# A straight first block with two low parts of weights in it, and a new share-out of the down projection's first low part

## The chip, the cores and the metric

The kernel runs on one core of one Trainium2 chip. The metric is device time in microseconds (us) of one execution; shown is the median of three. Engines: PE is TensorE, DVE is VectorE, ACT is ScalarE, POOL is GpSimd, SP is SyncE, which here only issues DMAs.

## The reference

One transformer block on x of shape (8, 1024, 512), with shared layernorm:

```python
    x = L0_attn_x
    xn = _layernorm(x, axis=-1)
    x = x + _L0_attn_ref(xn, L0_attn_Wq, L0_attn_Wk, L0_attn_Wv, L0_attn_Wog, L0_attn_Wig, L0_attn_big, L0_attn_Wfg, L0_attn_bfg, L0_attn_gamma, L0_attn_Wout) + _L0_ffn_ref(xn, L0_ffn_w_gate, L0_ffn_w_up, L0_ffn_w_down)
```

`_L0_attn_ref` is an mLSTM with 8 heads: q, k, v, an input and a forget gate from xn; a scan over the tokens of each sequence that updates a state C (32 x 64 a head) and a normalizer n with exponential gates under a running maximum; each head's output is normalized, multiplied by sigmoid(xn Wog) and gamma, and projected by Wout. `_L0_ffn_ref` is silu(xn w_gate) * (xn w_up), projected by w_down, with a hidden size of 2048. All in fp32.

## The kernel before

**Precision.** TensorE multiplies in fp16. Each fp32 operand is held as a sum of two fp16 numbers, a high part and a low part, and each product is three matrix products (high x high, high x low, low x high: L1127 to L1129 in `three`). So all weights have to be split once, in a prologue, before the loop over blocks can use them.

**The prologue.** The weights come in 17 pieces, in the order of `GROUPS`: gates, qk, v; g0 to g3 (gate projection); u0 to u3 (up); o; d0 to d3 (down); out. Each piece but gates has 128 x 2048 numbers. SyncE issues the loads. For each group VectorE takes the largest magnitude of each piece (`maximum`), the engines reduce it over the partitions, and `scales` makes a power of two from it. Then for each piece:

- ScalarE makes the high part, `high_part`: the weight times its scale, rounded to fp16 (L610; for `out` four pieces with their own factors, L607). It counts up `w_hi`.
- The low part, scaled weight minus high part, is made in one of three ways. On VectorE by one `scalar_tensor_tensor` that scales and subtracts (`low_part`, L811, L806 for `out`). On GpSimd for the pieces in `POOL_LOW` (`pool_low`, L508): GpSimd only subtracts, so for these ScalarE first scales the fp32 weight in place (L601) and then copies it to fp16 (L603). On TensorE for the pieces in `PE_LOW`: two products put scaled weight minus high part into four PSUM banks (`low_by_pe`, L1164, L1165), and ScalarE copies them out (`low_from_pe`, L616).

The order on each engine is the order of the code; engines meet by semaphores only. The fp32 weights are staged in memory that is free at the time: g in the slots of u, u in the slots of d, o in the slot of out, and d, qk, v and out in the arena, which holds the working tensors of the loop. This is why a piece of d may not be made before the piece of u that is staged in its slot is done (`wait_split` in `high_part`), and why before the loop VectorE, ScalarE and GpSimd wait for the last low part, that of `out`.

**The loop.** 32 blocks of 256 tokens, four to a sequence. Each engine has a loop of its own over the blocks (`Fori`), with its instructions in a fixed order. In a block TensorE computes gates, q, k, v, then 16 hidden pieces `ffn0` to `ffn15`, each with its gate and up product and, two pieces later, its down product (`down`). The table `AFTER` says which steps of the mLSTM come behind which piece: `es` the scores, `pv` their product with v and the state update, `center`, `scale` and `heads` the normalization of the output, `o` the output gate, `hoT` the turned output, `att` the projection by `out`. Three PSUM banks go round (`USES`, `BANK`): a product may begin when the use of its bank before has been drained. The first uses are gates, q, k; the next, v0, needs the bank of gates, which ScalarE (L656) and VectorE (L942) drain together. A hidden piece goes TensorE, ScalarE (tanh, L690), VectorE (L985, L988), ScalarE (high part, L694), GpSimd (low part, L560), TensorE (`down`).

Of the kernel before, what the change touches and what calls it, by code (L numbers as in the profile page):

```python
# [25 lines left out]
P = 128  # L26
# [98 lines left out]
POOL_LOW = [("qk", 0), ("v", 0), ("g", 0), ("g", 2), ("u", 0)]  # L125
PE_LOW = [("g", 1), ("g", 3), ("u", 1), ("u", 3)]
# [11 lines left out]
def low_done(piece):  # L138

    before = ORDER[:ORDER.index(piece) + 1]  # L140
    for own in (POOL_LOW, PE_LOW):
        if piece in own:
            return len([p_ for p_ in before if p_ in own])
    return len([p_ for p_ in before if p_ not in POOL_LOW and p_ not in PE_LOW])

# [24 lines left out]
def mlstm_mlp_kernel(nc, x, w_dram, gate_bias, gamma, out):  # L170
    ctx = ExitStack()
    with ctx:
# [92 lines left out]
        stage["out", 0] = in_arena(1)  # L265
# [36 lines left out]
        small = sb("small", [P, 112], F32)[:, :]  # L302
# [4 lines left out]
        m_carry = small[0:NH, 96:97]  # L307
        decay = small[:, 100:100 + NG * NCH].rearrange("p (g c) -> p g c", g=NG)
# [18 lines left out]
        w_in_place = sem("w_in_place")  # L327
        w_split = sem("w_split")
        w_split_pool = sem("w_split_pool")
        w_unscaled = sem("w_unscaled")  # L330
# [61 lines left out]
        def wait_split(eng, name, k):  # L392

            n = low_done((name, k))
            if (name, k) in POOL_LOW:
                eng.wait_ge(w_split_pool, n)
            elif (name, k) in PE_LOW:
                eng.wait_ge(w_split_act, n)
            else:
                eng.wait_ge(w_split, n)  # L400
# [27 lines left out]
        @block.sync  # L428
        def _(sp):
            sp.dma_start(xin, x_blocks[0, :, :, :]).then_inc(x_loaded, 16)  # L430
            sp.dma_start(bias[:, :], gate_bias).then_inc(small_loaded, 16)
            sp.dma_start(gam[:, :], gamma).then_inc(small_loaded, 16)
            for n, k in ORDER:
                if (n, k) == ("d", 3):

                    wait_split(sp, "qk", 0)
                if n == "out":

                    wait_split(sp, "v", 0)
# [12 lines left out]
        @block.gpsimd  # L452
        def _(pool):
# [86 lines left out]
            wait_split(pool, "out", 0)  # L540
# [46 lines left out]
        def _(act):  # L587
            s = nc.scalar

            def high_part(n, k):  # L590
# [8 lines left out]
                if (n, k) in POOL_LOW:  # L599
# [32 lines left out]
            for r, names in enumerate(GROUPS):  # L632
                act.wait_ge(w_scaled, r + 2 if names == ["out"] else r + 1)
# [4 lines left out]
                for n, k in pieces(names):  # L638
                    high_part(n, k)
                    if (n, k) == ("g", 3):  # L640
                        low_from_pe("g", 1)
                    elif (n, k) == ("u", 2):
                        low_from_pe("g", 3)
                    elif (n, k) == ("d", 0):
                        low_from_pe("u", 1)
                    elif (n, k) == ("d", 2):
                        low_from_pe("u", 3)
            act.wait_ge(w_unscaled, 1)
            act.wait_ge(state_ready, START)
            wait_split(act, "out", 0)  # L650

            with act.Fori(0, NB) as i:
# [32 lines left out]
                for j in range(NJ):  # L685
# [9 lines left out]
                    if j == 2:  # L695
                        act.wait_ge(rows_ready, i + 1)
                        s.activation(we[0:72, :], wr[0:72, :], ACT.Exp).then_inc(we_ready, 1)
                    for step in AFTER[j]:
# [39 lines left out]
                own.close()  # L738

        @block.vector  # L740
        def _(dve):
# [57 lines left out]
            def low_part(n, k):  # L799

                dve.wait_ge(w_hi, ORDER.index((n, k)) + 1)
                if n == "out":
                    for c in range(KC):
# [5 lines left out]
                    ins.then_inc(w_split, 1)  # L809
                    return  # L810
                d.scalar_tensor_tensor(out=low(n, k), in0=staged(n, k), scalar=wscale[:, sc[n]:sc[n] + 1],  # L811
                                       in1=high(n, k), op0=ALU.mult, op1=ALU.subtract).then_inc(w_split, 1)
# [88 lines left out]
            scales(4)  # L901
            link(d.tensor_scalar(unscale[:, NS + 1:NS + 2], unscale[:, NS + 1:NS + 2],
# [17 lines left out]
            wait_split(dve, "out", 0)  # L920
# [8 lines left out]
            with dve.Fori(0, NB) as i:  # L929
                own = Count(dve_own, DVE_OWN)  # L930

                def stack(h):

                    rows = slice(h * DQ, (h + 1) * DQ)
                    for n, (q_part, k_part) in enumerate(((0, 0), (1, 0), (0, 1))):
# [7 lines left out]
                                ALU.add).then_inc(free_of("gates"), 1)  # L943

# [36 lines left out]
                for j in range(NJ):  # L981
# [9 lines left out]
                    for step in DVE_AFTER[j]:  # L991
# [59 lines left out]
                        elif step.startswith("center"):  # L1051
                            dve.wait_ge(num_ready, START + i * 4 + 2 * k_ + 2)
# [67 lines left out]

        @block.tensor
        def _(pe):
# [46 lines left out]
            for r, names in enumerate(GROUPS):  # L1169
# [14 lines left out]
                elif names == ["out"]:  # L1184
                    low_by_pe("u", 3, range(KC))
            pe.wait_ge(w_split_act, len(PE_LOW))

            with pe.Fori(0, NB) as i:
# [39 lines left out]
                for j in range(NJ):  # L1228
# [20 lines left out]
                    for step in AFTER[j]:  # L1249
# [31 lines left out]
                        elif step in ("o0", "o1"):  # L1281
                            by_token(bank(step)[:, :], k, w_o).then_inc(work_full, 1)
# [62 lines left out]
```

## Time and profile before

| | us |
|---|---|
| median of 3 runs | 3085.51 |
| lowest and highest | 3082.91, 3086.01 |
| the profiled execution | 3083.87 |
| its span, first to last instruction | 3082.2 |
| PE busy | 3031.4 (98%) |
| DVE busy | 2385.5 (77%) |
| ACT busy | 1122.1 (36%) |
| POOL busy | 791.0 (26%) |

The profile is of one execution. Busy time is the time in which an engine executes something. A wait is given by the instruction that waited and by the one that released it. The prologue lasts until about 79 us; from there the blocks follow at 93.7 us each.

### The profile page before, as it was taken

To read this page: it belongs to the slowest core of one execution; us is meant where nothing else is said; L and a number is where in the kernel's file an instruction comes from. 1 tells how busy PE (TensorE), PEld (TensorE's weight loads), DVE (VectorE), ACT (ScalarE), POOL (GpSimd) and SP (SyncE) were. 2 spreads that over 40 slices of the span, in tenths; PEclk is the share of its full clock that TensorE was granted. 3 is DMA by queue.
4 is the path that set the end of the run, shared out by engine and by line. 5 is a ranking of instruction groups with operands and counts; after the bars stand their busy time and mean duration, and the time that the engine had idled before them with its cause. 6 is when DMAs were issued, how large, how long until landed. Compare 5 with 4: busy or idle time off the path is not lost.

```text
span 3082.2 us, 62629 instructions
## 1 busy us (share of the span) xinstructions
PE 3031.4 (98%) x22090; PEld 2196.6 (71%) x22090; DVE 2385.5 (77%) x6009; ACT 1122.1 (36%) x2160; POOL 791.0 (26%) x1122
## 2 busy tenths in 40 slices
PE   4999999999999999999999999999999999999999
PEld 2677777777777777777777777777777777777776
DVE  8877778877778877778777788777787777887777
ACT  7333333333333333333333333333233333333332
POOL 4222223222222222222222222222222222222222
PEclk9999999999999999999999999999999999999999
DMA  5000000000000000000000000000000000000000
GB/s 226 8 14 14 14 7 7 14 14 14 14 4 10 14 14 14 7 7 14 14 14 14 7 7 14 14 14 14 0 14 14 14 14 7 7 14 14 14 14 7
DMA packets 20334, 51.09 MB, mean 17 GB/s; under 512 B 1506, under 2 KB 1634, under 8 KB 18274
## 3 DMA queue, kind: packets, MB, share of 16 engines
q1 hardware_dynamic: 20322, 50.95, 4.4%
q8 instruction: 6, 0.10, 0.0%
q14 instruction: 6, 0.05, 0.0%
HBM read 34.16 MB, written 16.78 MB: 17 GB/s over the span
## 4 chain that ended last, share of the span: by engine, by line
PE 97%; DVE 1%; ACT 1%; issue 0%; DMA 0%; SPq 0%; ACTq 0%; DVEq 0%
PE work L1127 21%; PE work L1129 21%; PE work L1128 21%; PE acc L1129 7%; PE acc L1128 7%; PE acc L1127 7%; PE o_bank L1239 3%; PE o_bank L1291 2%; PE work L1297 2%; PE s_bank L1278 1%; PE work L1303 1%; PE e_bank L1272 1%; PE work L1216 1%; PE work L1164 0%; DVE amax L762 0%
## 5 line engine op out<-in xcount | busy, mean ns | idle before, releaser
L1127 PE MATMUL work<-xt,weights 128*128 128x256 f16 x4608 | 1256.0, 273 | 0.0
L1129 PE MATMUL work<-xt,weights 128*128 128x256 f16 x4608 | 1256.0, 273 | 0.0
L1128 PE MATMUL work<-xt,weights 128*128 128x256 f16 x4608 | 1255.9, 273 | 0.0
L560 POOL TENSOR_TENSOR arena<-arena 128x256 f16<-128x256 f32 x512 | 359.3, 702 | 1650.8 <-ACT arena L694 1650.8
L1127 PEld LDWEIGHTS work<-xt,weights 128*128 128x128 f16 x4608 | 478.5, 104 | 69.2
L1128 PEld LDWEIGHTS work<-xt,weights 128*128 128x128 f16 x4608 | 450.9, 98 | 69.6
L1129 PEld LDWEIGHTS work<-xt,weights 128*128 128x128 f16 x4608 | 450.8, 98 | 52.3
L694 ACT ACTIVATE arena<-arena 128x256 f16<-128x256 f32 x512 | 213.4, 417 | 727.5 <-DVE arena L988 727.5
L690 ACT ACTIVATE arena<-work,unscale 128x256 f32<-128x256 f32 x512 | 241.1, 471 | 548.6 <-PE work L1129 548.3
L1127 PE MATMUL acc<-weights,arena 128*128 128x512 f16 x1024 | 388.1, 379 | 0.5 <-POOL arena L560 0.5
L1128 PE MATMUL acc<-weights,arena 128*128 128x512 f16 x1024 | 388.1, 379 | 0.0
L1129 PE MATMUL acc<-weights,arena 128*128 128x512 f16 x1024 | 388.1, 379 | 0.0
L985 DVE SCALAR_TENSOR_TENSOR arena<-arena,work 128x256 f32<-128x256 f32 x512 | 215.7, 421 | 158.1 <-ACT arena L690 147.9
L829 DVE STREAM_TRANSPOSE arena<-arena 32x128 f32<-32x128 f32 x1024 | 309.7, 302 | 31.0
L550 POOL TENSOR_TENSOR pair_r<-arena,diag 40x1024 f16<-40x1024 f16 x64 | 133.8, 2091 | 487.0 <-DVE pair_l L971 487.0
L988 DVE SCALAR_TENSOR_TENSOR arena<-arena,work 128x256 f32<-128x256 f32 x512 | 215.3, 421 | 17.5
L1127 PE MATMUL work<-weights,xt 128*128 128x512 f16 x512 | 194.1, 379 | 2.4 <-DVE arena L942 1.6
L1128 PE MATMUL work<-weights,xt 128*128 128x512 f16 x512 | 194.0, 379 | 0.0
L1129 PE MATMUL work<-weights,xt 128*128 128x512 f16 x512 | 194.0, 379 | 0.0
L1129 PEld LDWEIGHTS acc<-weights,arena 128*128 128x128 f16 x1024 | 100.2, 98 | 120.8
L1239 PEld LDWEIGHTS o_bank<-arena 128*128 128x128 f32 x1024 | 164.6, 191 | 15.2
L1239 PE MATMUL o_bank<-arena 128*128 128x66 f32 x1024 | 171.2, 249 | 0.0
(215 smaller groups left out, 4105.4 us busy)
## 6 DMA issues: line engine op xcount, KB each, us to landing
arena<-x_dram SPq DMA_DIRECT2D x33, 512.0 KB, 3.3
out_dram<-arena SPq DMA_DIRECT2D x32, 512.0 KB, 2.8
weights<-w_g_dram SPq DMA_DIRECT2D x4, 1024.0 KB, 13.1
weights<-w_u_dram SPq DMA_DIRECT2D x4, 1024.0 KB, 20.6
arena<-w_d_dram SPq DMA_DIRECT2D x4, 1024.0 KB, 27.2
arena<-w_qk_dram SPq DMA_DIRECT2D x1, 1024.0 KB, 6.2
arena<-w_v_dram SPq DMA_DIRECT2D x1, 1024.0 KB, 8.2
weights<-w_o_dram SPq DMA_DIRECT2D x1, 1024.0 KB, 25.5
```

The lines of the kernel that those rows point to most:

```text
L550: g.tensor_tensor(pair_r[0:GR, :, :], uhl[0:GR, c * P:(c + 1) * P].unsqueeze(1).broadcast_to((GR, NH, P)), diag[0:GR, :].unsqueeze(2).broa ...
L560: g.tensor_tensor(hh[:, j % HB, 1, :], tt[:, j % 2, :], hh[:, j % HB, 0, :], ALU.subtract).then_inc(h_ready, 1)
L690: s.activation(tt[:, j % 2, :], bank(f"ffn{j}")[:, 0:BLOCK], ACT.Tanh, scale=unscale[:, sc["g"]:sc["g"] + 1]).then_inc(tanh_done, 1)
L694: s.activation(hh[:, j % HB, 0, :], tt[:, j % 2, :], ACT.Copy).then_inc(h_hi, 1)
L829: d.transpose(dst.rearrange("p (k t) -> p k t", k=KC)[r * 32:(r + 1) * 32, :, tokens], features).then_inc(xn_turned, 1)
L985: own.step(d.scalar_tensor_tensor(out=tt[:, j % 2, :], in0=tt[:, j % 2, :], scalar=1.0, in1=b[:, 0:BLOCK], op0=ALU.add, op1=ALU.mult))
L988: d.scalar_tensor_tensor(out=tt[:, j % 2, :], in0=tt[:, j % 2, :], scalar=HS, in1=b[:, BLOCK:2 * BLOCK], op0=ALU.mult, op1=ALU.mult).then_ ...
L1127: t.matmul(dst, w[0], a[0], start=first, stop=False, skip_group_check=True)
L1128: t.matmul(dst, w[0], a[1], start=False, stop=False, skip_group_check=True)
L1129: return t.matmul(dst, w[1], a[0], start=False, stop=last, skip_group_check=True)
L1239: mm_ = t.matmul(o_bank[:, k * VW:(k + 1) * VW], pm[:, UNIT_IN[j] % 2, k * P:(k + 1) * P], v[:, c, g * HG + k, :], start=False, stop=(k == ...
L1291: t.matmul(o_bank[:, 0:GW], qi[:, g, span], state[:, g, :], start=True, stop=False, skip_group_check=True)
```

## The change

Five edits go together.

1. u3's low part goes from TensorE to GpSimd. `PE_LOW` loses it, `POOL_LOW` gets it, so ScalarE makes u3 in two steps.
2. d0's low part goes from VectorE to GpSimd; here VectorE, not ScalarE, scales the fp32 piece in place, behind the scales of group d, and ScalarE copies.
3. The low parts of o and `out` and the high part of `out` go from the prologue into the first block: o's behind VectorE's part in draining gates, `out`'s high part on ScalarE behind hidden piece 9, its low part on VectorE in front of the second `center`. They count on a semaphore of their own, `w_split_late`, for which TensorE waits at each product with o and `out`.
4. For that, ScalarE's and VectorE's first block is written out as straight code, and their loops run over the other 31. TensorE, GpSimd and SyncE keep loops over 32.
5. `out` is staged in a tensor of its own, and its load no longer waits for v's low part. `small` is packed tighter to make room.

```diff
-POOL_LOW = [("qk", 0), ("v", 0), ("g", 0), ("g", 2), ("u", 0)]
-PE_LOW = [("g", 1), ("g", 3), ("u", 1), ("u", 3)]
+POOL_LOW = [("qk", 0), ("v", 0), ("g", 0), ("g", 2), ("u", 0), ("u", 3), ("d", 0)]
+PE_LOW = [("g", 1), ("g", 3), ("u", 1)]
+LATE_LOW = [("o", 0), ("out", 0)]
...
-        stage["out", 0] = in_arena(1)
+        stage["out", 0] = sb("stage_out", [P, SLOT], F32)[:, :]
...
-                if n == "out":
-
-                    wait_split(sp, "v", 0)
...
-            wait_split(pool, "out", 0)
+            pool_low("u", 3)
+            pool_low("d", 0)
+            wait_split(pool, "d", 3)
...
-                if (n, k) in POOL_LOW:
+                if (n, k) == ("d", 0):
+
+                    act.wait_ge(d_in_place, 1)
+                    s.activation(high(n, k), w, ACT.Copy).then_inc(w_hi, 1)
+                elif (n, k) in POOL_LOW:
...
-                    elif (n, k) == ("d", 2):
-                        low_from_pe("u", 3)
             act.wait_ge(w_unscaled, 1)
             act.wait_ge(state_ready, START)
-            wait_split(act, "out", 0)
-
-            with act.Fori(0, NB) as i:
+            wait_split(act, "d", 0)
+            wait_split(act, "d", 3)
+
+            def act_block(i, first):
...
+                    if first and j == 9:
+                        act.wait_ge(w_scaled, len(GROUPS) + 1)
+                        high_part("out", 0)
...
+            act_block(0, True)
+            with act.Fori(1, NB) as i:
+                act_block(i, False)
+
...
             scales(4)
+            d.tensor_scalar(stage["d", 0], stage["d", 0], wscale[:, sc["d"]:sc["d"] + 1], None,
+                            ALU.mult).then_inc(d_in_place, 1)
...
-            low_part("o", 0)
-            for n in range(4):
+            for n in range(1, 4):
                 low_part("d", n)
-            low_part("out", 0)
+            wait_split(dve, "d", 0)
...
+                if first:
+                    low_part("o", 0)
 
                 dve.wait_ge(log_f_ready, i + 1)
...
                         elif step.startswith("center"):
+                            if first and k_ == 1:
+                                low_part("out", 0)
...
+            dve_block(0, True)
+            with dve.Fori(1, NB) as i:
+                dve_block(i, False)
+
...
-                elif names == ["out"]:
-                    low_by_pe("u", 3, range(KC))
...
                     wait_drained(pe, i, f"hoT{c}")
+                    wait_split(pe, "out", 0)
...
                         elif step in ("o0", "o1"):
+                            wait_split(pe, "o", 0)
```

**ScalarE, from piece u3 to the first block, before.** L610 is a high part in one step (u3, o, d0, d1, d2, d3 in this order), L616 a copy of a low part made by TensorE (u1, then u3), L607 the high part of `out`.

```order
L610 ACTIVATE weights<-weights,wscale 128x2048 [waits w_split_act]
L610 ACTIVATE weights<-weights,wscale 128x2048 [waits w_scaled]
L610 ACTIVATE weights<-arena,wscale 128x2048 [waits w_split_pool,w_scaled]
L616 ACTIVATE weights<-work0 128x512 [waits w_low_full]
...
L610 ACTIVATE weights<-arena,wscale 128x2048 [waits w_split_act]
L610 ACTIVATE weights<-arena,wscale 128x2048 [waits w_split]
L616 ACTIVATE weights<-work0 128x512 [waits w_low_full]
...
L610 ACTIVATE weights<-arena,wscale 128x2048 [waits w_split_act]
L607 ACTIVATE weights<-arena,out_scale 128x512 [waits w_split,w_scaled]
```

**The same place in the changed program.** L609 and L611 are the two steps of u3, L618 is the one-step form, L606 the copy of d0, L624 the copies of u1's low part, L663 the first instruction of the first block.

```order
L609 ACTIVATE weights<-weights,wscale 128x2048 [waits w_split_act]
L611 ACTIVATE weights<-weights 128x2048 [waits w_in_place]
L618 ACTIVATE weights<-weights,wscale 128x2048 [waits w_scaled]
L606 ACTIVATE weights<-arena 128x2048 [waits d_in_place,w_split_pool,w_scaled]
L624 ACTIVATE weights<-work0 128x512 [waits w_low_full]
...
L618 ACTIVATE weights<-arena,wscale 128x2048 [waits w_split_act]
L618 ACTIVATE weights<-arena,wscale 128x2048 [waits w_split]
L618 ACTIVATE weights<-arena,wscale 128x2048 [waits w_split_pool]
L663 ACTIVATE arena<-work0 40x256 [waits w_split,w_split_pool,work_full,state_ready,w_unscaled]
```

u3 has one instruction more, d0 waits for VectorE's scale, the four copies of u3's low part and the four instructions of `out` are gone from here, and d3 now waits for GpSimd.

**VectorE, from the scales of group d to the first block, before.** L811 is a low part in one step: u2, later o and d0 to d3.

```order
L796 TENSOR_SCALAR wscale<-wscale 128x1 [waits dve_set]
L902 TENSOR_SCALAR unscale<-unscale,pow2 128x1 [waits w_scaled]
L904 TENSOR_SCALAR unscale<-unscale 128x1 [waits dve_set]
L811 SCALAR_TENSOR_TENSOR weights<-weights,wscale 128x2048 [waits w_hi,dve_set]
...
L811 SCALAR_TENSOR_TENSOR weights<-weights,wscale 128x2048 [waits w_hi]
L811 SCALAR_TENSOR_TENSOR weights<-arena,wscale,weights 128x2048 [waits w_hi] x4
L806 SCALAR_TENSOR_TENSOR weights<-arena,out_scale,weights 128x512 [waits w_hi] x4
L929 UNCONDITIONAL_BRANCH [waits w_split,state_ready,w_unscaled]
L929 ISA
L942 TENSOR_TENSOR arena<-work0,arena 40x256 [waits gates_low]
L946 TENSOR_SCALAR arena<-arena 8x256 [waits log_f_ready]
```

**The same place in the changed program.** L917 is the scale of d0 in place, L825 the low part in one step, L958 the first instruction of the first block.

```order
L810 TENSOR_SCALAR wscale<-wscale 128x1 [waits dve_set]
L917 TENSOR_SCALAR arena<-arena,wscale 128x2048 [waits w_scaled]
L919 TENSOR_SCALAR unscale<-unscale,pow2 128x1
L921 TENSOR_SCALAR unscale<-unscale 128x1 [waits dve_set]
L825 SCALAR_TENSOR_TENSOR weights<-weights,wscale 128x2048 [waits w_hi,dve_set]
...
L825 SCALAR_TENSOR_TENSOR weights<-arena,wscale,weights 128x2048 [waits w_hi] x3
L958 TENSOR_TENSOR arena<-work0,arena 40x256 [waits w_split,state_ready,gates_low,w_unscaled,w_split_pool]
L825 SCALAR_TENSOR_TENSOR weights<-weights,wscale 128x2048 [waits w_hi]
L964 TENSOR_SCALAR arena<-arena 8x256 [waits log_f_ready]
```

The scale of d0 came in front, d0's own low part left, o's low part moved behind the first instruction of the block, the four of `out` further into it, and the branch into the loop is gone from here.

## Rows read from the trace of the kernel before

**Rows 1.** Stages: us, busy PE, PEld, DVE, ACT, POOL, PE clock, DMA, GB/s.

```profile
79.30:173.00 93.70, 90.33 (x650) 64.11 (x651) 72.63 (x187) 33.17 (x67) 24.22 (x35) 1.00 0.02 7
...
1000.00:1094.00 94.00, 94.00 (x691) 68.42 (x690) 72.45 (x185) 33.66 (x67) 23.96 (x33) 1.00 0.03 11
...
61.50:66.00 4.50, 2.46 (x6) 1.24 (x7) 3.86 (x9) 4.47 (x7) 0.00 (x0) 0.81 0.00 0
66.00:70.00 4.00, 4.00 (x10) 1.35 (x8) 4.00 (x3) 1.69 (x1) 0.00 (x0) 0.79 0.00 0
```

**Rows 2.** Waits of PE from 79 to 175 us: total, times, longest.

```profile
PE work L1127 <- DVE arena L942: 1.6, 1, 1.6
PE s_bank L1278 <- DVE arena L938: 0.9, 1, 0.9
PE work L1127 <- ACT arena L667: 0.8, 1, 0.8
PE acc L1127 <- POOL arena L560: 0.5, 1, 0.5
```

**Rows 3.** Timeline of PE, its first product of block 0: start, duration.

```profile
72.59 1.04 PE L1216 MATMUL work<-xt,parts_gates 128*128 128x256 f16 x8 [2.45 <-ACT weights L616]
```

**Rows 4.** Timeline of DVE, end of the prologue; idle before in brackets.

```profile
60.26 2.35 DVE L811 SCALAR_TENSOR_TENSOR weights<-weights,wscale 128x2048 f16<-128x2048 f32 x1
...
66.63 6.87 DVE L811 SCALAR_TENSOR_TENSOR weights<-arena,wscale,weights 128x2048 f16<-128x2048 f32 x3
...
76.58 2.73 DVE L806 SCALAR_TENSOR_TENSOR weights<-arena,out_scale,weights 128x512 f16<-128x512 f32 x4
80.00 0.42 DVE L942 TENSOR_TENSOR arena<-work,arena 40x256 f32<-40x256 f32 x1 [0.69 <-ACT arena L656]
83.26 0.28 DVE L946 TENSOR_SCALAR arena<-arena 8x256 f32<-8x256 f32 x1 [2.84 <-ACT arena L665]
```

**Rows 5.** Timeline of ACT, prologue.

```profile
46.35 1.91 ACT L603 ACTIVATE weights<-weights 128x2048 f16<-128x2048 f32 x1
...
54.02 3.89 ACT L610 ACTIVATE weights<-weights,wscale 128x2048 f16<-128x2048 f32 x2
59.82 2.00 ACT L610 ACTIVATE weights<-arena,wscale 128x2048 f16<-128x2048 f32 x1 [1.91 <-DVE wscale L796]
61.73 1.55 ACT L616 ACTIVATE weights<-work 128x512 f16<-128x512 f32 x3
...
74.19 2.54 ACT L607 ACTIVATE weights<-arena,out_scale 128x512 f16<-128x512 f32 x4
79.59 0.38 ACT L656 ACTIVATE arena<-work 40x256 f32<-40x256 f32 x1 [2.86 <-DVE weights L806]
```

**Rows 6.** Timeline of POOL: a low part of the prologue, and two places in blocks.

```profile
48.40 4.08 POOL L508 TENSOR_TENSOR weights<-weights 128x2048 f16<-128x2048 f32 x1 [1.99 <-ACT weights L603]
...
148.77 0.87 POOL L560 TENSOR_TENSOR arena<-arena 128x256 f16<-128x256 f32 x1 [4.57 <-ACT arena L694]
...
182.42 1.89 POOL L550 TENSOR_TENSOR pair_r<-arena,diag 40x1024 f16<-40x1024 f16 x1 [15.38 <-DVE pair_l L971]
```

**Rows 7.** Timeline of DVE at the same places in blocks 0 and 1.

```profile
149.15 0.78 DVE L1049 TENSOR_SCALAR arena<-arena,keep 128x528 f32<-128x528 f32 x1
152.75 0.69 DVE L1053 TENSOR_REDUCE small<-arena 128x8 f32<-128x512 f32 x1 [2.82 <-ACT arena L716]
...
176.00 0.28 DVE L946 TENSOR_SCALAR arena<-arena 8x256 f32<-8x256 f32 x1 [2.84 <-ACT arena L665]
...
182.38 2.48 DVE L975 SCALAR_TENSOR_TENSOR arena<-arena,unscale 128x512 f16<-128x512 f32 x1
```

**Rows 8.** Timeline of ACT and of DVE at hidden piece 10 of block 0.

```profile
135.63 0.47 ACT L690 ACTIVATE arena<-work,unscale 128x256 f32<-128x256 f32 x1 [0.62 <-PE work L1129]
...
137.55 0.42 DVE L985 SCALAR_TENSOR_TENSOR arena<-arena,work 128x256 f32<-128x256 f32 x1
```

**Rows 9.** DMA issues: KB each, us from issue to landing.

```profile
arena<-w_gates_dram SPq DMA_DIRECT2D x1, 80.0 KB, 3.3
```

More of the change, by code:

```diff
@@ L140, in low_done @@
     before = ORDER[:ORDER.index(piece) + 1]
-    for own in (POOL_LOW, PE_LOW):
+    for own in (POOL_LOW, PE_LOW, LATE_LOW):
         if piece in own:
             return len([p_ for p_ in before if p_ in own])
-    return len([p_ for p_ in before if p_ not in POOL_LOW and p_ not in PE_LOW])
+    return len([p_ for p_ in before if p_ not in POOL_LOW and p_ not in PE_LOW and p_ not in LATE_LOW])
 START = 1
@@ L301, in mlstm_mlp_kernel @@
         wtok = at["wtok"].rearrange("p (c r) -> p c r", c=NCH)
-        small = sb("small", [P, 112], F32)[:, :]
+        small = sb("small", [P, 92], F32)[:, :]
         bn6 = small[:, 0:12].rearrange("p (c s) -> p c s", c=NCH)
@@ L306, in mlstm_mlp_kernel @@
         hsum, mu, den, rden, vsum, var, rd, fac = (small[:, 24 + 8 * n:32 + 8 * n] for n in range(8))
-        m_carry = small[0:NH, 96:97]
-        decay = small[:, 100:100 + NG * NCH].rearrange("p (g c) -> p g c", g=NG)
+        m_carry = small[0:NH, 20:21]
+        decay = small[:, 88:88 + NG * NCH].rearrange("p (g c) -> p g c", g=NG)
         work = [pb(f"work{n}") for n in range(3)]
@@ L327, in mlstm_mlp_kernel @@
         w_in_place = sem("w_in_place")
+        d_in_place = sem("d_in_place")
         w_split = sem("w_split")
         w_split_pool = sem("w_split_pool")
+        w_split_late = sem("w_split_late")
         w_unscaled = sem("w_unscaled")
@@ L398, in wait_split @@
                 eng.wait_ge(w_split_act, n)
+            elif (name, k) in LATE_LOW:
+                eng.wait_ge(w_split_late, n)
             else:
@@ L631, in _ @@
                 x_high(0, c, (e_bank, s_bank)[c][:, :])
-            for r, names in enumerate(GROUPS):
-                act.wait_ge(w_scaled, r + 2 if names == ["out"] else r + 1)
+            for r, names in enumerate(GROUPS[:-1]):
+                act.wait_ge(w_scaled, r + 1)
                 if names in (["g"], ["u"]):
@@ L808, in low_part @@
                                                      op0=ALU.mult, op1=ALU.subtract)
-                    ins.then_inc(w_split, 1)
+                    ins.then_inc(w_split_late, 1)
                     return
                 d.scalar_tensor_tensor(out=low(n, k), in0=staged(n, k), scalar=wscale[:, sc[n]:sc[n] + 1],
-                                       in1=high(n, k), op0=ALU.mult, op1=ALU.subtract).then_inc(w_split, 1)
+                                       in1=high(n, k), op0=ALU.mult,
+                                       op1=ALU.subtract).then_inc(w_split_late if n == "o" else w_split, 1)
             def stats(step):
@@ L913, in _ @@
                             1.0 / (WS * OS * 2), None, ALU.mult).then_inc(w_unscaled, 1)
-            low_part("o", 0)
-            for n in range(4):
+            for n in range(1, 4):
                 low_part("d", n)
-            low_part("out", 0)
+            wait_split(dve, "d", 0)
             dve.wait_ge(w_unscaled, 1)
             dve.wait_ge(state_ready, START)
-            wait_split(dve, "out", 0)
+            wait_split(dve, "d", 3)
             def add_mlstm(i, c):
@@ L927, in add_mlstm, with dve_block @@
                                        op0=ALU.mult, op1=ALU.add).then_inc(free_of(f"att{c}"), 1)
-            with dve.Fori(0, NB) as i:
+            def dve_block(i, first):
                 own = Count(dve_own, DVE_OWN)
```

## The prediction

> **What bounds the kernel now.** I read the busy time of each engine by stage first. In a steady block TensorE is busy for all of the 94 us, at a granted clock of 1.00 [rows 1], which is the upper of its two levels, 2.4 GHz. The steady blocks give nothing to win unless TensorE's own work shrinks, and the change leaves that alone. What is left is the prologue, and the first block, in which TensorE is idle for 3.4 us of 93.7 [rows 1]. So the time is "when TensorE can go on with the first block", plus 32 blocks that it bounds itself.
>
> The waits of TensorE in the first block [rows 2] name the places: 1.6 us for VectorE at L942, which drains the gates' bank; 0.8 us for ScalarE at L667; 0.5 us for GpSimd's low part of the first hidden piece; 0.9 us for VectorE's stacks (L938). TensorE had begun the block at 72.59 [rows 3] and had gates, q and k done before it stopped. It stopped because ScalarE and VectorE were still in the prologue. VectorE ran one low part after another, three from 66.63, a fourth, and the four pieces of `out` from 76.58, which end at 79.31 [rows 4]. ScalarE waited for that last one (2.86 us idle) and drained gates at 79.59 [rows 5]; VectorE followed at 80.00. The quantity that the change moves is therefore this 79.31: the moment at which both are free for the block. Everything in the first block hangs on it.
>
> **The profiled execution** took 3083.87 us around a span of 3082.2; the median of the runs is 3085.51, that is 1.6 more. I take the difference that I work out off the median.
>
> **The change part by part, on ScalarE.** (1) Piece u3 gets the two-step form: scaled in place, then copied. ScalarE's two pieces at 54.02 took 3.89, 1.95 each [rows 5], and behind them it was idle for 1.91 until the scale of `d` was there at 59.82. A copy costs 1.91 (L603). So u3 now runs 54.0 to 56.0 and 56.0 to 57.9, and o to 59.9: the new copy fills the idle time and costs 0.1 us. (2) TensorE's low part of u3 and its four copies by ScalarE go (three took 1.55 at 61.73, with the fourth about 2.1). (3) d0 must wait for VectorE's in-place scale and is then a copy, 1.91. (4) The 2.54 us for `out` [rows 5] leave the prologue.
>
> **On GpSimd**, a low part begins 2.05 us after ScalarE's copy has begun (46.35 to 48.40) and takes 4.08 [rows 5, 6]. For u3 that is 58.1 to 62.1.
>
> **On VectorE**, the new in-place scale of d0 can be issued at 59.8. No row shows it at 2048 columns. Its own cost is bounded from L946, 0.28 for 256 columns, and L1049, which is 0.78 for 528 [rows 7]. The second seems too slow beside the first, and the reason decides this prediction: GpSimd's L560 ran from 148.77 to 149.64 [rows 6], L1049 began at 149.15 and ended 0.29 after it. The same is seen at 182.4: GpSimd's L550 lasts 1.89, VectorE's L975 began 0.04 earlier and took 2.48, ending 0.55 after it [rows 6, 7]; its 512 columns are a quarter of L811's 2048, which take 2.29 [rows 4], so 0.57 is its own work. I read this as one of the two holding the other off. Then 528 columns cost 0.29 of their own, and 2048 some 1.1. The lower bound of the step is 1.1, the upper one 1.1 behind the end of GpSimd's u3: 62.1 + 1.1 = 63.2, or 3.4 after 59.8. I take the upper one, since L1049 is the nearest row in kind.
>
> The Trainium skill says so too, and more broadly (GPSIMD Engine Reference, Key points): GpSimd shares its SBUF interfaces with VectorE, and contends with instructions in a two-port mode or with two SBUF inputs. An fp32 scalar operation from SBUF is in such a mode by its page VectorE: DVE Perf Modes (Mode 2×_2P), so the rule speaks against this change; by it the step ends at 63.2, as the rows say, and without it at 60.9. The trace agrees for L1049 by 0.29 us; it has no such scale of 2048 columns.
>
> From there: ScalarE copies d0 to 65.1, takes in u1's low part to 67.2, and makes d1 by 69.2, d2 by 71.1, d3 by 73.1. VectorE has two small steps (0.4) and then u2's low part, 2.35 [rows 4], from 63.7 to 66.0. GpSimd's d0 could begin at 65.3; held by u2's low part it begins at 66.0 and ends at 70.1. VectorE's d1 has two SBUF inputs, so although d1 is ready at 69.2 it begins at 70.1. Three low parts took 6.87 [rows 4]: 70.1 + 6.9 = 77.0. **Against 79.3 that is 2.3 us earlier.** What was removed in front, o's low part, d0's and the four of `out`, is 2.35 + 2.35 + 2.73 = 7.4 us of VectorE, and 1.1 is added; of the 6.3 left, 4.0 is lost to waiting for GpSimd and for the copies.
>
> **What moves into the first block.** o's low part (2.35) stands behind L942, where VectorE waited 2.84 for ScalarE's logarithm [rows 4]: hidden with 0.5 to spare, and if it weren't, the chain behind it would be late by up to 2.35. The low parts of `out` (2.73) stand before the second `center`, in front of L1053, where VectorE was idle for 2.82 [rows 7]: hidden with 0.1 to spare. ScalarE's 2.54 for `out` come behind the tenth hidden piece, shortly before the tanh at 135.63; that tanh ends up at about 137.6 and lasts 0.47. VectorE did not take it up before 137.55 [rows 8], so VectorE is some 0.5 late there, with idle time of its own behind. TensorE didn't wait anywhere in that stretch [rows 2]. I charge nothing, and 1 us at most. The waits of TensorE for the low parts of o and `out` ride on matrix products that wait already; they repeat in all 32 blocks. Steady TensorE shows no idle time in spite of dozens of such waits [rows 1], so nothing for them. The straight copy of the first block drops register work; at most 0.2 us.
>
> **TensorE** now enters the block behind u1's copies, at 67.2 + 0.3 = 67.5. Gates, q and k took 6.3 us, from 72.59 to where 1.6 us before 80.48 it stopped [rows 2, 3]. It had been nearly idle since 61.5, so it may begin at 1.2 GHz: before, such a restart shows means of 0.81 over 4.5 us and 0.79 over 4 [rows 1], together 3.4 us at the lower level, worth 1.7 us. 67.5 + 6.3 + 1.7 = 75.5, still before the drain at 77.0 + 1.2 = 78.2. Hidden, and it costs 1.7 only where that cover is gone.
>
> **The sum:** 3085.5 - 2.3 = **3083.2 us**. This is 0.07%; a measurement of this kernel tells about 0.2%, 6.2 us, from no change. The three runs of before alone spread over 3.1.
>
> **The rivals.**
> *A, the forecast* (0.60): two holds by GpSimd, 2.3 us gained, with 1.5 to 3.5 as its own width: 3082.0 to 3084.0.
> *B, GpSimd holds VectorE's scale off less* (0.20). For it: L1049 is one form, in place of a proof, and some small VectorE steps ran beside GpSimd's low parts in the prologue. Then the scale ends at 60.9, d0's copy at 62.8, d1 is ready at 66.9, and GpSimd's d0, held by u2's low part until 63.7, ends at 67.8: 67.8 + 6.9 = 74.7, 4.6 us gained. With no hold at all VectorE begins d1 at 66.9 and is done at 73.8, 5.5 gained. Times of 3080.0 to 3080.9.
> *C, the gain is given back in the first block* (0.13). TensorE waits 2.7 us for the drain now, and if the clock drops there, v and the first hidden pieces run at half speed for those 3.4 us, 1.7 us lost, before the 0.8, 0.5 and 0.9 of waits that can absorb it [rows 2]. With ScalarE's lateness by up to 1 us on top, the result is a gain of 0 to 1.5: 3084.0 to 3085.5. Against it: this slack is larger than the loss.
> *D, slower* (0.05). VectorE's loop now stands behind a straight copy of a block and is entered or repeated at another place in its code. If each turn had to fetch code again, VectorE would be late at L942 in each block. The nearest row for a small fetch is the 80 KB load, 3.3 us to landing [rows 9]. In block 0 VectorE's chain starts 2.8 after TensorE's v (83.26 against 80.48), and in a steady block before it; the slack decides, and it is about 2 us. From there each us counts 31 times: 1.3 x 31 = 40 us, 3125. Against it: the loop itself is as long as before.
> The last 0.02 is for what I haven't seen.
>
> **How the numbers follow.** A, B and C end within 6.2 us, save for B's far end with an unlucky median (0.06 for faster with the unseen). Slower by over 6.2 is D and the rest: 0.06. Within: 0.88. For the range, A to C span 3080.0 to 3085.5; half the 3.1 spread on either side gives 3078.5 to 3087.
>
> **What the profile of the changed kernel would show.** If A holds: VectorE's scale of d0 (L917) reads about 3.4 us long, from 59.8, and ends about 1.1 after GpSimd's second-last low part; GpSimd's last low part reads over 4.5; ScalarE is idle for 3.3 before d0's copy; d1's low part is longer than d2's or starts late; ScalarE's L663 is at 77.3; TensorE's wait before v is again 1 to 3 us; the four pieces of `out` (L820) stand in front of the second `center`, which has no idle time left before its reduction. B: a scale of 1.1 to 1.3 us. C: a TensorE wait or a clock under 1.00 between 78 and 110. D: idle VectorE at each block's start, and a steady block above 93.7. Wrong most easily: the length of the two holds, 2.3 us each, and whether VectorE or GpSimd goes first when both are ready.

## The result: 3.65% slower, all of it in the loop and none of it in what the change was about

The changed kernel takes 3195.97 us (median of 4 runs, 3195.28 to 3196.36), the kernel before 3084.21 beside it (4 runs). The ratio is 1.0365, with a 95% interval of 1.0352 to 1.0378. The profiled execution has a span of 3194.2 us at a granted clock of 0.997, and of 1.00 in the steady stage below, so TensorE's clock isn't the reason.

The page of the changed kernel, its busy times and its DMA queues (packets, MB, share):

```profile
span 3194.2 us, 62566 instructions
...
PE 3059.0 (96%) x22078; PEld 2181.2 (68%) x22078; DVE 2389.3 (75%) x6009; ACT 1102.3 (35%) x2157; POOL 793.0 (25%) x1124
...
q14 instruction: 158, 1.29, 0.1%
q8 instruction: 6, 0.10, 0.0%
```

The last two rows count packets that bring instructions. The page of the kernel before has 6 packets on q14; here it has 158, of 8.2 KB each (1.29 MB by 158). The stages, with the columns of [rows 1]:

```profile
77.00:170.00 93.00, 91.86 (x655) 64.95 (x656) 77.36 (x191) 35.37 (x71) 23.98 (x33) 0.98 0.02 7
1000.00:1097.00 97.00, 93.96 (x683) 67.06 (x683) 72.04 (x184) 32.12 (x65) 23.23 (x33) 1.00 0.03 11
```

In [rows 1] TensorE was busy for 94.00 of the 94.00 us at this place. Now it is idle for 3.0 of 97.0. Two rows of the waits show where it begins (total, times, longest):

```profile
ACT arena L666 <- DVE arena L958: 163.2, 32, 5.6
DVE arena L958 <- issue: 139.8, 30, 4.9
```

and TensorE's own, from 300 to 3100 us, where the kernel before has none at all:

```profile
PE s_bank L1301 <- DVE arena L954: 24.8, 28, 0.9
PE work L1151 <- ACT arena L674: 21.2, 28, 0.8
PE work L1151 <- DVE arena L958: 17.1, 29, 0.8
PE acc L1151 <- POOL arena L564: 15.7, 28, 0.6
```

L958 is the drain of the gates' bank, L942 before. VectorE waited there 30 times, 4.7 us each, "for issue": for nothing that the profile shows on another engine. There are 31 turns of its loop and 30 jumps back. TensorE's four waits are those of the first block in [rows 2], at the same four places: now each block begins late, as only the first one did. VectorE at one such place, start, duration and idle time before:

```profile
555.49 0.75 DVE L1137 SCALAR_TENSOR_TENSOR arena<-acc,unscale,arena 128x512 f32<-128x512 f32 x1
560.93 0.41 DVE L958 TENSOR_TENSOR arena<-work,arena 40x256 f32<-40x256 f32 x1 [4.68 <-issue]
564.18 0.28 DVE L964 TENSOR_SCALAR arena<-arena 8x256 f32<-8x256 f32 x1 [2.84 <-ACT arena L672]
```

L1137 is the last instruction of a turn and L958 the first of the next. Where the straight copy runs on into the loop, with no jump back, there is no gap:

```profile
168.64 0.75 DVE L1137 SCALAR_TENSOR_TENSOR arena<-acc,unscale,arena 128x512 f32<-128x512 f32 x1
169.31 0.40 DVE L958 TENSOR_TENSOR arena<-work,arena 40x256 f32<-40x256 f32 x1
```

The same operation of block 1 stood at 172.75 before. So at the end of block 0 the changed kernel was 3.4 us *ahead*, and lost it and 112 us more in the 30 jumps. The chain at one jump (start, duration, what). It counts from the jump itself, some 0.6 before L1137 ends, so it has 5.2 us, and they fall into two pieces:

```profile
554.71 0.76 DVE arena L941
555.64 2.80 issue
558.49 2.44 issue
560.93 0.43 DVE arena L958
561.38 0.61 ACT arena L666
```

The prologue is the part that the prediction worked out. VectorE, against [rows 4]:

```profile
59.89 2.48 DVE L917 TENSOR_SCALAR arena<-arena,wscale 128x2048 f32<-128x2048 f32 x1
...
62.71 2.35 DVE L825 SCALAR_TENSOR_TENSOR weights<-weights,wscale 128x2048 f16<-128x2048 f32 x1
...
66.49 2.53 DVE L926 TENSOR_SCALAR out_scale<-gam,wscale 128x4 f32<-128x4 f32 x1
...
69.13 6.87 DVE L825 SCALAR_TENSOR_TENSOR weights<-arena,wscale,weights 128x2048 f16<-128x2048 f32 x3
76.69 0.42 DVE L958 TENSOR_TENSOR arena<-work,arena 40x256 f32<-40x256 f32 x1 [0.70 <-ACT arena L663]
77.04 2.33 DVE L825 SCALAR_TENSOR_TENSOR weights<-weights,wscale 128x2048 f16<-128x2048 f32 x1
79.96 0.28 DVE L964 TENSOR_SCALAR arena<-arena 8x256 f32<-8x256 f32 x1 [0.59 <-ACT arena L672]
```

GpSimd, against [rows 6]:

```profile
57.22 4.06 POOL L510 TENSOR_TENSOR weights<-weights 128x2048 f16<-128x2048 f32 x1 [0.53 <-ACT weights L611]
64.48 4.52 POOL L510 TENSOR_TENSOR weights<-arena,weights 128x2048 f16<-128x2048 f32 x1 [3.19 <-ACT weights L606]
```

VectorE is through with the low parts at 69.13 + 6.87 = 76.0, 3.3 us earlier than the 79.31 of [rows 4]. Some 0.8 of that isn't the change's: ScalarE's first copies of TensorE's low part of g3 stand at 41.25 against 42.04 before, with the same instructions in front, and in the run with 8 memsets below they stand at 42.45. Counted from these copies VectorE is through after 37.3 us before, and after 34.7 in both changed kernels: 2.5 us is what the change gains.

### The profile page after: what moved, and what is told of

Read it like the earlier page. It is cut to its first block, busy times and chain, and to the rows that moved or that the text cites. A ratio compares the mean times of both kernels' runs of the same rounds, so it can differ in the third digit from the quotient of the medians.

```text
span 3194.2 us, 62566 instructions
## 1 busy us (share of the span) xinstructions
PE 3059.0 (96%) x22078; PEld 2181.2 (68%) x22078; DVE 2389.3 (75%) x6009; ACT 1102.3 (35%) x2157; POOL 793.0 (25%) x1124
## 3 DMA queue, kind: packets, MB, share of 16 engines
q14 instruction: 158, 1.29, 0.1%
## 4 chain that ended last, share of the span: by engine, by line
PE 67%; DVE 20%; issue 12%; ACT 2%; DMA 0%; DVEq 0%; SPq 0%; ACTq 0%
PE work L1153 13%; PE work L1152 13%; PE work L1151 13%; PE acc L1151 6%; PE acc L1153 6%; PE acc L1152 6%; DVE arena L953 3%; DVE arena L954 3%; PE o_bank L1262 3%; DVE arena L993 2%; PE o_bank L1315 2%; PE work L1321 2%; DVE arena L1003 2%; PE s_bank L1301 1%; DVE arena L1006 1%
## 5 line engine op out<-in xcount | busy, mean ns | idle before, releaser
L554 POOL TENSOR_TENSOR pair_r<-arena,diag 40x1024 f16<-40x1024 f16 x64 | 127.0, 1985 | 629.8 <-DVE pair_l L989 629.8
```

Source lines behind the costliest of these rows:

```text
L554: g.tensor_tensor(pair_r[0:GR, :, :], uhl[0:GR, c * P:(c + 1) * P].unsqueeze(1).broadcast_to((GR, NH, P)), diag[0:GR, :].unsqueeze(2).broa ...
```

## The experiments

**Number and place of instructions.** Every instruction of VectorE has a record in the trace, register work and branches too. Counting them from the first one, which is 0, gives an instruction's place in VectorE's program, as far as no record is missing. The loop body has 290 instructions in every kernel here. It runs from 115 to 404 in the kernel before, and from 318 to 607 in the changed one, because the straight copy stands ahead of it. "A turn" is the mean distance between VectorE's jumps back: 93.74 us before, 97.59 in the changed kernel. 3.85 x 30 = 115.5 us, which with 3.3 gained is the 112 lost.

**1. Everything but VectorE's straight block.** VectorE loops over all 32 blocks again, with the low parts of o and `out` back in the prologue (and ScalarE's high part of `out`); the rest of the change stays.

```diff
-            dve_block(0, True)
-            with dve.Fori(1, NB) as i:
-                dve_block(i, False)
+            with dve.Fori(0, NB) as i:
+                dve_block(i, False)
```

> The changed kernel, but VectorE loops over all 32 blocks again; the low parts of o and out are made by VectorE, and the high part of out by ScalarE, at the end of the prologue. ScalarE's first block stays straight, all waits on w_split_late stay, and GpSimd keeps u3 and d0. Theory 1 (VectorE fetches its loop's code again at each turn because the straight block stands in front of it): no idle time of 'issue' before L958, some six instruction packets behind the prologue, a block period of 93.7 us, and VectorE free for the block at about 76.0 + 2.3 + 2.7 = 81.0, so 3085.5 + 1.7 = 3087, against 3196 for the changed kernel. Theory 2 (the new waits of TensorE, ScalarE's straight block or GpSimd's new low parts cost the 3.9 us a block): a period near 97.7 stays, 3196 or more.

Measured: 3085.38 us (3083.93 to 3086.77), ratio 1.0005, interval 0.9996 to 1.0015, a turn of 93.74, 6 packets on q14. The loss is gone. ScalarE's straight block, which stayed, costs nothing that can be measured.

**2. Nothing but VectorE's straight block.** The kernel before, with this edit alone:

```diff
-            with dve.Fori(0, NB) as i:
+            def dve_block(i):
...
+            dve_block(0)
+            with dve.Fori(1, NB) as i:
+                dve_block(i)
```

> The kernel before with one edit: VectorE's first block as straight code, its loop over the other 31. Nothing is computed elsewhere. Theory 1: it alone brings the idle time of 4.7 us before the first VectorE instruction of each block from block 2 on, a period of 97.7 and a time near 3085 + 30 x 4.0 = 3205. Theory 2: 3085.

Measured: 3199.18 us, a turn of 97.61, 158 packets. The row of the waits reads

```profile
DVE arena L942 <- issue: 140.3, 30, 4.9
```

So the straight block is needed for the loss and is enough for it. The low parts, GpSimd's work and the semaphores have no share. It doesn't yet say why: the copy could hurt through the length of the program, or through where it puts the loop.

**3 and 4. Length and place without a straight block.** The kernel before, with 60 or 150 memsets of one element at the head of VectorE's program, while it would wait for the input:

```diff
+            for n in range(60):
+                d.memset(filler[0:1, n:n + 1], 0.0)
             dve.wait_ge(x_loaded, 16)
```

> The kernel before with 60 memsets of one number each in front of VectorE's program, the loop as it was. VectorE's program grows from about 405 to 465 instructions. Theory 1a (the loop is fetched again once the whole program is over 512 instructions): period 93.7, about 3085 plus what the fillers delay the prologue (2 to 8 us). Theory 1b (it is fetched again when the loop spans too many of the 128-instruction packets, whatever the program's length: from instruction 175 it spans fewer than before): 93.7 too. Theory 1c (a straight copy of the block is needed for it): 93.7.

> The kernel before with 150 such memsets: VectorE's program has about 555 instructions, and its loop begins at 265. Theory 1a: the period rises to 97.7, 3085 + 120 + 5 to 15 for the fillers. Theory 1c (only a straight copy of the block does it): 93.7, and only the fillers' 5 to 15 us are lost.

Measured: 3132.77 us with 60 (a turn of 95.23, 162 packets), and 3082.4 with 150 (93.74, 7 packets, the program being longer). More instructions, no loss. So it isn't the length, and it needs no straight copy: 60 instructions that do nothing of use cost 49 us, and 90 more give them back. None of the three theories had foreseen a turn above 93.74 with 60 memsets. 1a and 1c are refuted by these two runs. 1b counted on fewer packets at 175; where the boundaries lie was read from the trace afterwards. Nor were the 5 to 15 us for the fillers to be seen: 3082.4 is no more than the kernel before. In the trace of 60 memsets the stall is shorter:

```profile
555.97 0.75 DVE L1120 SCALAR_TENSOR_TENSOR arena<-acc,unscale,arena 128x512 f32<-128x512 f32 x1
558.94 0.42 DVE L945 TENSOR_TENSOR arena<-work,arena 40x256 f32<-40x256 f32 x1 [2.22 <-issue]
```

**The theory that came of it.** Where packets come late, there are five per turn, and each can be set against the instruction that VectorE had reached. Both have two behind the jump back. In the changed kernel the rest come as VectorE passes the places 320, 447 and 577; with 60 memsets, the places 190, 318 and 450. The distances are 127 to 132: packets hold some 128 instructions, with boundaries near 64, 192, 320, 448, 576 and 704. The loop of 290 touches three packets in a good place and four in a bad one. Theory: three stay loaded from turn to turn, four don't, and then each jump back waits for code. The stall is long where the loop begins just ahead of a boundary, since the next packet is needed at once too. In the changed kernel that is 2 instructions ahead, and the chain above has two pieces, 2.80 and 2.44; with 60 memsets it is 17 ahead, and one piece of 2.73 is left. The records of the packets show it directly. At the jump of the changed kernel shown above (555.58) they run from 556.59 to 557.10 and from 559.06 to 559.59. The first instruction of the turn, a register operation, stands at 558.44, behind the first packet; L958, the second instruction, stands at 560.93, behind the second. With 60 memsets (jump at 556.05, packets 557.06 to 557.54 and 559.46 to 560.00) L945 stands at 558.94, before the second packet is even there.

The Trainium skill (Runtime: NRT & Kernel Launch, Instruction fetch mechanics) states the mechanism: a taken branch whose target isn't in the loaded window must fetch before execution goes on. The trace agrees on that, with 4.7 us. It has the window as two pages of 256 instructions, in blocks of 16 KiB. Worked out from that figure, as an estimate, a loop of 290 touches a third page only where it begins in the last 33 places of one. The loops that stall in the runs below begin at 165, 175, 318 and 438, which is 165, 175, 62 and 182 within 256: no place of the pages fits all four. The trace has packets of 8.2 KB on q14; here the measurement decides.

**5 to 8. The theory put to the test at new places.** The changed kernel with 8 and with 120 memsets, the kernel before with 84, and the changed kernel with 8 memsets and without the second half of the change. The memsets now write scratch columns that are overwritten later, as there was no room for a tensor of their own.

```diff
+            for n in range(8):
+                d.memset(small[n // 64 * 32:n // 64 * 32 + 1, 24 + n % 64:25 + n % 64], 0.0)
             dve.wait_ge(x_loaded, 16)
```

> The changed kernel with 8 one-element memsets ahead of VectorE's program, nothing else. Theory (place of the loop against the packets of its code): VectorE's loop stands 8 instructions further on, so that it touches three packets of 128 instructions and not four. No code is fetched from 80 us on (6 packets of VectorE's instruction queue in all, as in the kernel before, not 158), no idle time put down to issue before L958, a turn of 93.74 us, and what is left of the change is its prologue, 3.3 us earlier than before: about 3081, between 3079.5 and 3083.5. Rival (length of VectorE's program, or the straight copy of a block as such): 3196, a turn of 97.6. Rival (some other part of the change slows a steady block): a turn between the two.

> The changed kernel with 120 such memsets. Theory of the place: the loop begins some 120 instructions later, at 438 by the records, just ahead of the next boundary at about 448, so that it touches four packets again: 5 packets of 8 KB a turn, idle time put down to issue at the back branch, a turn above 95, a time of 3130 to 3200. Rival (any shift away from where the loop stood cures it; the boundary does not come round again): 3081.

> The kernel before with 84 such memsets: its program is longer than with 60, which cost 49 us, and shorter than with 150, which cost nothing. Theory of the place: the loop runs from 199 to 488 by the records and touches three packets (boundaries at about 192, 320, 448, 576): 3084, a turn of 93.74, 6 packets. Rival (a band of program lengths that is bad, whatever the place within 128): between 3110 and 3140.

Measured: the changed kernel with 8 memsets takes **3080.5 us** (3079.53 to 3081.56, 11 runs) against 3083.14 for the kernel before (21 runs), ratio 0.9991, interval 0.9982 to 1.0000. Eight instructions more make it 115 us faster. The same stage of its trace has TensorE without a gap:

```profile
1000.00:1097.00 97.00, 97.00 (x715) 70.62 (x713) 74.44 (x192) 33.86 (x67) 25.02 (x34) 1.00 0.03 11
```

With 120 memsets it takes 3123.54, a turn of 95.19, and

```profile
DVE arena L960 <- issue: 68.2, 30, 2.5
```

The kernel before with 84 takes 3086.18, with a turn of 93.74. In loss or no loss all three came out as the theory of the place has it. Three details did not. The changed kernel with 8 memsets has 8 packets and not 6, the last at 247 us, so code is still fetched in the first turns. With 84 there are 7 and not 6. And 3123.54 lies below the 3130 to 3200 that was expected with 120. The rivals "length", "the copy as such", "any shift cures it" and "a band of lengths" each fail at one of them.

**9 and 10. How sharp the edge is.** The kernel before with 40 and with 50 memsets, so that the loop ends 4 short of the boundary at 448, or 6 past it.

> The kernel before with 40 memsets ahead of VectorE's program. The loop runs from 155 to 444 by the records. Theory (a loop that touches four packets of 128, with boundaries near 64, 192, 320, 448, is fetched again at each turn; one that touches three is not): it ends 4 short of the boundary at about 448, three packets, 3084, a turn of 93.74, no late packets. Rival (the loss depends on something else that grows between 0 and 60 memsets): part of the 49 us that 60 cost, 3090 or more.

> The kernel before with 50 memsets. The loop runs from 165 to 454 and crosses the boundary at about 448: four packets. Theory: code is fetched at each turn, some 158 late packets. Its beginning has 27 instructions left in the first packet, more than with 60 memsets (17), so the stall behind the back branch is 2.2 us or less and the time 3100 to 3133. Rival: 3084, as with 40.

Measured: 3083.31 us and 6 packets with 40; 3130.55, 162 packets and

```profile
DVE arena L944 <- issue: 70.8, 31, 2.5
```

with 50. Ten memsets cost 47 us. The stall, 2.28, is a little above the 2.2 that was expected; 10 instructions more in the first packet didn't shorten it. All kernels together, each counted from its trace (packets touched by boundaries at 64 + a multiple of 128):

```
kernel                            loop        packets   stall   turn     time
                                  from..to    touched   each
before                            115..404    3         0       93.74    3084.21
changed, VectorE's loop over 32   116..405    3         0       93.74    3085.38
before + 40 memsets               155..444    3         0       93.74    3083.31
before + 84                       199..488    3         0       93.74    3086.18
before + 150                      265..554    3         0       93.74    3082.4
changed + 8                       326..615    3         0       93.74    3080.5
changed + 8, d0 low by VectorE    326..615    3         0       93.74    3078.49
before + 50                       165..454    4         2.28    95.21    3130.55
before + 60                       175..464    4         2.31    95.23    3132.77
changed + 120                     438..727    4         2.27    95.19    3123.54
changed                           318..607    4         4.66    97.59    3195.97
before, straight block alone      318..607    4         4.68    97.61    3199.18
```

In this table the stall is the total of the waits for issue by their number (68.2 / 30 and so on). Stall less loss per turn is 0.81 or 0.82 us in the three short cases and 0.81 in the changed kernel (4.66 - 3.85). That is VectorE's slack at its jump back.

**The number of packets.** It follows from the place, in all twelve kernels. VectorE's program brings in one packet for each boundary that it passes, and in the bad places five more for each jump back; three others come in every kernel, within its first 202 us and whatever its place. Before, boundaries 64, 192 and 320 are passed: 3 + 3 = 6. Changed + 8 passes 448 and 576 too: 5 + 3 = 8. Changed: 5 + 3 + 5 x 30 = 158. With 50 or 60 memsets: 4 + 3 + 5 x 31 = 162. With 120: 6 + 3 + 150 = 159. The five at a jump are one more than the four that the loop touches: in the changed kernel the last is fetched at about 577, 30 places before the loop ends and with the next boundary at 704. So it looks as if each boundary calls for the packet behind the next one, and as if four packets are held, three of the loop and the one ahead. That is worked out from the counts; no run reads what is held.

**The second half of the change by itself.** The changed kernel with 8 memsets, but with no scale of d0 in place and with d0's low part by VectorE:

```diff
-POOL_LOW = [("qk", 0), ("v", 0), ("g", 0), ("g", 2), ("u", 0), ("u", 3), ("d", 0)]
+POOL_LOW = [("qk", 0), ("v", 0), ("g", 0), ("g", 2), ("u", 0), ("u", 3)]
...
-            d.tensor_scalar(stage["d", 0], stage["d", 0], wscale[:, sc["d"]:sc["d"] + 1], None,
-                            ALU.mult).then_inc(d_in_place, 1)
...
-            for n in range(1, 4):
+            for n in range(4):
                 low_part("d", n)
```

> The changed kernel with 8 memsets, and the second half of the change undone: no scale of d0 in place by VectorE, its low part by VectorE again and not by GpSimd, ScalarE makes d0's high part in one step. Theory (GpSimd's low part holds VectorE's scale, and the hand-over to GpSimd and back costs more than it saves): VectorE is done with the low parts at 73.5 to 74.5 us, not 76.0, and the time is 1.5 to 2.5 us below the run with 8 memsets alone, about 3079. Rival (GpSimd's help is worth its price): VectorE is done at 76 or later, and the time is the same or 1 to 2 us above.

Measured: **3078.49 us** (3077.89 to 3080.33, 11 runs), ratio 0.9986, interval 0.9977 to 0.9995, the fastest kernel of the study and 2.0 below the one with 8 memsets alone. Its VectorE:

```profile
57.42 5.03 DVE L820 SCALAR_TENSOR_TENSOR weights<-weights,wscale 128x2048 f16<-128x2048 f32 x1
...
64.09 0.23 DVE L921 TENSOR_SCALAR out_scale<-gam,wscale 128x4 f32<-128x4 f32 x1
...
64.42 9.13 DVE L820 SCALAR_TENSOR_TENSOR weights<-arena,wscale,weights 128x2048 f16<-128x2048 f32 x4
```

It is through at 64.42 + 9.13 = 73.55, 2.5 before the changed kernel's 76.0 and 3.6 before the 77.2 with 8 memsets alone. Not all of that is the edit's. ScalarE's copies of g3's low part, which stand ahead of anything the edit touches, are at 40.27 in this execution, against 41.25 and 42.45. Counted from there VectorE is through after 33.3 us, against 34.7 in the other two: 1.5 us. The runs of the two kernels overlap (3077.89 to 3080.33 and 3079.53 to 3081.56), but their medians differ by more than chance gives, 2.0 us with an interval of 0.6 to 2.5. The hand-over of d0 to GpSimd costs more than the one low part that it saves. GpSimd's low part of u3 (56.23 to 60.30 here) still holds VectorE, only now its low part of u2, which reads 5.03 and not 2.35.

## Why the prediction was wrong

It said 3083.2 us, and 0.88 for no change that can be told; 3195.97 came.

**The step that failed** is the first one: "The steady blocks give nothing to win unless TensorE's own work shrinks, and the change leaves that alone", with the time as "when TensorE can go on with the first block", plus 32 blocks that it bounds itself. This holds for gains. For losses it needs VectorE to be on time in each block, and its slack there is 0.8 us.

**Rival D was the case that came**, with a chance of 0.05. What stood against it, "the loop itself is as long as before", was true and beside the point: its length is 290 instructions in all kernels, and its place decides (runs 2 to 10). By place, the twelve kernels of the table show a loss in five. By the rule of the table a loop of 290 touches four packets from 33 of the 128 places where it can begin, one in four, so 0.05 was too low for a change that moves the loop by 203 places. I had priced D at 3.3 us a fetch less 2 of slack, 1.3 x 31 = 40 us. Measured in the changed kernel it is 4.66 less 0.81, 3.85 x 30 = 115.5 (31 turns have 30 jumps). Both terms were off: two waits one behind the other instead of one, and a slack less than half of what I read from block 0. The single late fetch of the runs with 50, 60 and 120 memsets (2.27 to 2.31) is below the 3.3 of [rows 9], and its loss, 1.45 to 1.49 a turn, is near the 1.3 of D by luck: the fetch was taken 1.0 too long and the slack 1.2 too long.

**The other steps held**, as the changed kernel and its form with 8 memsets show:
- *VectorE's scale of d0 held by GpSimd*: predicted to end 1.1 after GpSimd's low part of u3. It ended at 59.89 + 2.48 = 62.37, 1.09 after 57.22 + 4.06 = 61.28. It reads shorter than the forecast 3.4 because GpSimd began earlier. In the run with 8 memsets it reads 3.36.
- *GpSimd's d0*: forecast from 66.0, held by u2's low part, with more than 4.5 on the page. It is 4.52 long from 64.48 in the record, with u2's low part from 62.71 to 65.06 beside its beginning. That low part reads its usual 2.35, so GpSimd was the one held, by some 0.46 over its 4.06. The end is 69.0 against 70.1.
- *Three low parts to 77.0*: 76.0, and the 0.8 from TensorE's earlier work explains most of the difference. With 8 memsets the last one ends at 77.2.
- *o's low part hidden* in L946's wait of 2.84: L964 still waits 0.59 behind it. *`out` hidden before the second `center`*: 2.73 long, then L1073 with 0.20 of its wait left, 0.1 forecast.
- *The gain*: forecast 2.3, in the run with the loop in a good place 2.6 (3083.14 - 3080.5, interval 0 to 5.5), and 2.5 in the prologue counted from g3's copies. The size came out as worked out, but the time alone doesn't tell it from nothing.
- *Rival C's mechanism was there and cost nothing that reached the end.* From 75 to 80 us the granted clock is 0.66, in the changed kernel, so part of this stretch ran at 1.2 GHz, behind TensorE's wait of 2.74 for the drain. Block 1 begins 3.4 us early all the same: the slack took it, as the text had against C.

```profile
75.00:80.00 5.00, 2.83 (x7) 1.04 (x8) 3.71 (x4) 3.15 (x6) 0.27 (x2) 0.66 0.00 0
```

**What is shown and what is argued.** Shown: the loss comes with the place of VectorE's loop and goes with 8 instructions; the edge lies between 444 and 454 for its end; late packets and waits for issue come together, in twelve kernels out of twelve. Argued: that three packets are kept and a fourth isn't. The rule fits all twelve, in loss and in the number of packets, but no run changes the length of the loop, so a threshold in its length is open. Open too is whether the other engines' loops have such places: none of them showed a wait of this kind in any run. ScalarE's loop has 139 instructions and GpSimd's 62, too few to touch four packets of 128 anywhere; TensorE's has over 750 and shows none either, so the rule isn't TensorE's. The kernels of the table that were run once aren't told apart within 6 us; those with 8 memsets have 11 runs each.

## What to carry to other kernels

A change that adds or drops instructions ahead of a hardware loop on one engine can move the time by several per cent through the place of the loop alone. When every turn has a wait "for issue" behind the jump back and the page counts a packet of instructions per turn or more, shift the loop by some instructions at the head of the program before judging the change. Judge a peeled block with its loop in a good place: here that turned a loss of 3.65% into a gain of 0.09%, with an interval of 0 to 0.18%. And an engine that isn't the bound has a slack in each block that can be measured; a small lateness beyond it is paid in every turn.

## What the runs showed of the hardware that I had not expected

- VectorE's instructions come in packets of 8.2 KB, some 128 instructions. A loop of 290 that touches four of them has five packets fetched in each turn, and VectorE waits 2.3 us at each jump back, or 4.7 where the loop begins 2 instructions ahead of a packet's end.
- GpSimd's low part (two inputs from SBUF, 128x2048) holds off more of VectorE than the large operations. The 128x4 scale of `out_scale` reads 2.53 us in the changed kernel and ends with GpSimd's low part, at 69.0; with GpSimd idle it reads 0.23. Operations of 128x1 between them (66.11 and 66.30) took 0.16 and 0.15. The low part of u2 took 5.03, ending 2.15 after GpSimd's, and 2.35 where GpSimd was idle. The page that the prediction drew on, GPSIMD Engine Reference of the Trainium skill (Key points), says that the two share the interfaces, and the trace agrees; that the operation which began first runs to its end is what these rows add: GpSimd's here, and u2's low part over GpSimd's d0 in the changed kernel.
